# Routed layers of a transformer kernel: router products summed in one instruction, norm behind the gather, value blocks and head-wise exponentials on ScalarE, scores without key blocks

## The reference

```
weights = (x @ router_w)[..., 0] + router_b[0]            # (8, 512)
topv, topi = top_k(weights, 64); thr = topv[:, -1]
sel_mask = weights > thr
sel_idx = sort(topi[:, :63])                              # 63 tokens of each sequence
x_sel, pos_sel, w_sel, m_sel = the same tokens of x, position_ids, weights, attention_mask
hn = rmsnorm(x_sel, ln1)
q, kk, v = rope(heads(hn @ wq)), rope(heads(hn @ wk)), heads(hn @ wv)     # 16 heads of 16
a = softmax(q kk^T / 4 + m_sel)
x1 = x_sel + (a v) @ wo
x2 = x1 + gelu(rmsnorm(x1, ln2) @ w1) @ w2
out = x2 * w_sel at the selected places, 0 elsewhere, + x * (1 - sel_mask)
x = x_before + 0.5 * out
```

## Time and profile before

| | us |
|---|---|
| median of 3 runs | 2997.37 (2995.15 to 2999.2) |
| the profiled execution's own time | 3000.29 |
| its span in the profile | 2998.6 |
| first routed layer, from the first statistics to the last scatter addition | 1591.8 to 1814.4 |
| second routed layer, first block's places to the second norm | 2826.3 to 2944.3 |
| TensorE busy | 2496.2 |
| VectorE busy | 2165.9 |
| ScalarE busy | 1512.2 |
| GpSimd busy | 841.5 |

### The profile page before, as it was taken

One profiled execution on the slowest core, in us unless ns is written; L12 is line 12 of the kernel. 1 busy time (PEld: TensorE's weight loads), 2 busy tenths in 40 slices (PEclk: granted clock), 3 DMA queues, 4 the chain that ended last, 5 costly groups with the idle time before them and its releaser, 6 DMA issues. The chain is left out here.

```text
span 2998.6 us, 38823 instructions
## 1 busy us (share of the span) xinstructions
PE 2496.2 (83%) x13889; PEld 1335.8 (45%) x13889; DVE 2165.9 (72%) x3838; ACT 1512.2 (50%) x2213; POOL 841.5 (28%) x820
## 2 busy tenths in 40 slices
PE   6999999999899989899991576688888888885256
PEld 3444444444444444344440344355555555554134
DVE  3389688878889887979107564688878978873765
ACT  5655554546455545555551121377766766772111
POOL 3444343544444434444440000102211211221000
PEclk9999999999999999999995776799999999997678
DMA  5000000000000000000001001000000000001001
GB/s 162 24 1 1 1 1 1 1 1 1 1 1 1 1 1 1 1 1 1 1 1 48 15 1 36 1 2 2 2 3 2 2 3 2 1 2 49 14 1 57
DMA packets 29459, 33.07 MB, mean 11 GB/s; under 512 B 6568, under 2 KB 25704, under 8 KB 29272
## 3 DMA queue, kind: packets, MB, share of 16 engines
q1 hardware_dynamic: 28296, 28.02, 2.9%
q0 software_dynamic: 976, 2.56, 0.3%
HBM read 25.72 MB, written 4.19 MB: 10 GB/s over the span
## 5 line engine op out<-in xcount | busy, mean ns | idle before, releaser
L716 POOL TENSOR_TENSOR g_lo<-g_full,g_hi 128x512 f16<-128x512 f32 x512 | 658.4, 1289 | 912.0 <-ACT g_hi L788 910.4
L788 ACT ACTIVATE g_full<-hid,b_col 128x512 f32<-128x512 f32 x512 | 351.4, 686 | 562.1 <-PE hid L152 560.6
L150 PE MATMUL hid<-y_hi,w_hi 128*128 128x512 f16 x1024 | 396.3, 387 | 37.6 <-DVE y_lo L774 34.9
L151 PE MATMUL hid<-y_lo,w_hi 128*128 128x512 f16 x1024 | 395.7, 386 | 0.0
L152 PE MATMUL hid<-y_hi,w_lo 128*128 128x512 f16 x1024 | 395.2, 386 | 0.0
L150 PE MATMUL acc<-g_hi,w_hi 128*128 128x512 f16 x1024 | 389.2, 380 | 0.0
L151 PE MATMUL acc<-g_lo,w_hi 128*128 128x512 f16 x1024 | 389.1, 380 | 0.0
L152 PE MATMUL acc<-g_hi,w_lo 128*128 128x512 f16 x1024 | 388.9, 380 | 0.0
L788 ACT ACTIVATE g_hi<-hid,b_col 128x512 f16<-128x512 f32 x512 | 348.6, 681 | 0.0
L2027 DVE TENSOR_REDUCE mla_m_col<-mla_ps 128x1 f32<-128x512 f32 (+3 forms) x512 | 225.2, 484 | 66.1 <-PE mla_ps L1869 60.0
L2130 ACT ACTIVATE mla_p_full<-mla_ps 128x1280 f32<-128x1280 f32 x128 | 158.3, 1237 | 143.8 <-PE mla_ps L1899 143.5
(11 more groups left out here) (369 smaller groups left out, 4781.6 us busy)
## 6 DMA issues: line engine op xcount, KB each, us to landing
stage<-in_L_ffn_w_dram SPq DMA_DIRECT2D x16, 512.0 KB, 4.9
x<-in_L_attn_x_dram SPq DMA_DIRECT2D x8, 512.0 KB, 8.4
routed_w<-in_L_ffn_w_dram SPq DMA_DIRECT2D x4, 1024.0 KB, 8.5
out_dram<-x SPq DMA_DIRECT2D x8, 512.0 KB, 5.7
mla_sums<-mla_sum_row SPq DMA_DIRECT2D x128, 2.0 KB
mla_wq<-in_L_attn_Wq_dram SPq DMA_DIRECT2D x1, 1024.0 KB, 6.8
mla_wout<-in_L_attn_Wout_dram SPq DMA_DIRECT2D x1, 1024.0 KB, 9.1
routed_wqkv<-in_L_ffn_wq_dram SPq DMA_DIRECT2D x2, 256.0 KB, 3.7
```

The costliest lines, as they stand in the source:

```text
L150: pe.matmul(out, w_hi, v_hi, start=first, stop=False)
L151: pe.matmul(out, w_hi, v_lo, start=False, stop=False)
L716: pool.tensor_tensor(g_lo[:, g, :], g_full[:, g, :], g_hi[:, g, :], ALU.subtract).then_inc(tail_done, 1)
L788: act.activation(out[:, g, :], hid[:, ht % 4, :], ACT.Gelu, bias=b1_col[:, ht:ht + 1], scale=1.0 / WS).then_inc(gelu_done, 1)
```

## The change

In both routed layers:

- **Weighing.** VectorE multiplies the centred tile by the router column and sums it in one instruction (`accum_out`), 32 times, and multiplies the 32 sums by `rstd` afterwards. ScalarE normalizes all 32 tiles.
- **Blocks.** The first block ends with the copies of `slot_col` and `stay`. `one_hot`, the gather, the transposes of `one_hot` and the whole mask part move into the second block. GpSimd now zeroes `v_blk` and `qk` there and then issues the four mask gathers.
- **Norms.** Square and sum are taken pair by pair, right behind the copy of that pair's rows (first norm) or behind `add_selected` (second norm).
- **Order.** Values are projected before queries and keys, into shared banks. The mask pieces stand between the query and key projections on TensorE and between the rotations on VectorE.
- **Value blocks** are 16 ScalarE copies.
- **No key blocks.** `rotate` writes each head into a group of 32 rows with zeros in the other half; `turn_qk` makes eight transposes for a pair instead of four, both results are copied by ScalarE. `scores` makes 32 products for a pair, each of 16 rows by 64 columns.
- **Softmax.** The subtraction is gone: VectorE negates the maxima, ScalarE takes 16 exponentials of 64 elements for a pair with the maximum as bias and the sum as accumulated output. `softmax_shift` drains four banks of 256 elements; `scores` has one set of banks and waits for that drain.

Core of the diff:

```diff
-                    with dve.Fori(0, BATCH // 2) as two:
...
-                            dve.tensor_tensor(weighed[:, i, :, :], y[:, b, :, 0:D],
-                                              router[:, :].unsqueeze(1).to_broadcast([P, TILES, D]),
-                                              ALU.mult).then_inc(weigh_step, 1)
...
-                            dve.tensor_reduce(w_col[:, b, :], weighed[:, i, :, :], AX.X, ALU.add).then_inc(weigh_step, 1)
+                            if col >= 4:
+                                dve.wait_ge(weigh_step, col - 3)
+                            dve.scalar_tensor_tensor(weighed[:, t, :], x[:, b, t, :], ln_col[:, 3, col:col + 1], router[:, :],
+                                                     ALU.subtract, ALU.mult,
+                                                     accum_out=w_col[:, b, t:t + 1]).then_inc(weigh_step, 1)
+                    dve.tensor_tensor(flat_w, flat_w, rstd[:, :], ALU.mult).then_inc(weigh_step, 1)
...
+        def rms_square(dve, call, pr, src):
+            at = call * RMS_STEPS + 2 * pr
+            dve.tensor_tensor(sq[:, pr, :], src[:, pr, :], src[:, pr, :], ALU.mult).then_inc(rms_step, 1)
             dve.wait_ge(rms_step, at + 1)
+            dve.tensor_reduce(col[:, 0, pr:pr + 1], sq[:, pr, :], AX.X, ALU.add).then_inc(rms_step, 1)
...
         def scores(pe, pr):
+            if pr == 0:
+                pe.wait_ge(rot_step, 8 * PAIRS)
+            else:
+                pe.wait_ge(s_step, 6 * (pr - 1) + 4)
+            pe.wait_ge(qkt_out, 2 * (pr + 1))
+            for m in range(BLOCKS):
+                for i in range(2):
+                    toks = slice(i * ROWS, (i + 1) * ROWS)
+                    for c in range(4):
+                        rows = slice(32 * c, 32 * c + HEAD_DIM)
+                        last = pe.matmul(ps[toks, S_BANK + c, m * ROWS:(m + 1) * ROWS],
+                                         qk_t[rows, pr, m, toks], qk_t[rows, pr, BLOCKS + m, toks],
+                                         start=True, stop=True)
+            last.then_inc(s_done, 1)
...
-            dve.tensor_tensor(sv, sv, mx.unsqueeze(2).to_broadcast([P, HEADS, ROWS]), ALU.subtract).then_inc(s_step, 1)
+            dve.tensor_scalar(mx, mx, -1.0, None, ALU.mult).then_inc(s_step, 1)
...
             for m, (a, table) in enumerate(((0, cos), (1, sin), (0, sin), (1, cos))):
                 dve.tensor_tensor(r[m], src[:, :, a, :], table, ALU.mult).then_inc(rot_step, 1)
-            dve.tensor_tensor(out[:, :, 0, :], r[0], r[1], ALU.subtract).then_inc(rot_step, 1)
-            dve.tensor_tensor(out[:, :, 1, :], r[2], r[3], ALU.add).then_inc(rot_step, 1)
+            for a in range(2):
...
+                dve.tensor_tensor(out[:, :, :, 0:half], parts[0], parts[1], ALU.subtract).then_inc(rot_step, 1)
+                dve.tensor_tensor(out[:, :, :, half:2 * half], parts[2], parts[3], ALU.add).then_inc(rot_step, 1)
...
                 def exponential(pr):
-                    act.wait_ge(s_step, 4 * (pr + 1))
-                    act.activation(s[:, pr % 2, :, :], s[:, pr % 2, :, :], ACT.Exp).then_inc(s_exp, 1)
+                    act.wait_ge(s_step, 6 * (pr + 1))
+                    for hd in range(HEADS):
+                        last = act.activation(s[:, pr % 2, hd, :], s[:, pr % 2, hd, :], ACT.Exp,
+                                              bias=s_col[:, pr % 2, 0, hd:hd + 1],
+                                              accum_out=s_col[:, pr % 2, 1, hd:hd + 1])
+                    last.then_inc(s_exp, 1)
```

More of the change, by code:

```diff
@@ L1007, in _ @@
                     dve.wait_ge(small_in, 48)
-                    dve.tensor_copy(pos_rows_f[:, :], pos_rows[:, :]).then_inc(hot_step, 1)
-                    with dve.Fori(0, BATCH) as b:
+                    dve.tensor_copy(pos_rows_f[:, :], pos_rows[:, :]).then_inc(col_out, 1)
+                    for b in range(BATCH):
                         for t in range(TILES):
@@ L1193, in routed_layer @@
         proc_lo = sb("proc_lo", [P, PAIRS, D], F16)
+        hot_step = sem("hot_step")
+        gathered = sem("gathered")
+        sel_out = sem("sel_out")
+        hot_turned = sem("hot_turned")
+        hot_out = sem("hot_out")
+        mask_in = [keep.software(nc.semaphore(f"{tag}_mask_in{i}")) for i in range(PAIRS)]
+        mask_turned = sem("mask_turned")
+        mask_out = sem("mask_out")
+        mask_picked = sem("mask_picked")
+        mask_done = sem("mask_done")
         rms_step = sem("rms_step")
@@ L1273, in routed_layer, with select @@
         ANG_STEPS = 1 + 16
-        S_BANK, W_BANK = (6, 0, 6, 0), (2, 4, 2, 4)
+        QK_BANK = (3, 4, 5, 6)
+        V_BANK = (7, 7, 0, 0)
+        TURN_BANK = ((7, 0), (1, 2), (7, 0), (1, 2))
+        S_BANK = 3
         PUT_BANK = (2, 4, 6, 0)
-        def turn_qk(pe, pr):
-            pe.wait_ge(rot_step, 6 * (pr + 1))
-            for m in range(4):
-                last = pe.transpose(ps[:, 2 + pr, m * P:(m + 1) * P], qk[:, pr % 2, m * P:(m + 1) * P], ident[:, :])
+        def select(pe, pr):
+            for i in range(2):
+                for t in range(TILES):
+                    last = pe.matmul(ps[i * ROWS:(i + 1) * ROWS, 3 + pr, 0:ROUTED_EXT],
+                                     one_hot[:, pr, t, i, :], y[:, 2 * pr + i, t, :],
+                                     start=(t == 0), stop=(t == TILES - 1))
+            last.then_inc(gathered, 1)
@@ new lines, in turn_hot, with project_values @@
+        def turn_hot(pe, pr):
+            for t in range(TILES):
+                last = pe.transpose(ps[:, (7, 0)[pr % 2], t * P:(t + 1) * P],
+                                    one_hot[:, pr, t, :, :].rearrange("p i r -> p (i r)"), ident[:, :])
+            last.then_inc(hot_turned, 1)
+        def project_values(pe, pr):
+            for k in range(KD):
+                last = pe.matmul(ps[:, V_BANK[pr], (pr % 2) * D:(pr % 2 + 1) * D], h_t[:, k, pr * P:(pr + 1) * P],
+                                 wqkv[:, k, 2 * D:QKV], start=(k == 0), stop=(k == KD - 1))
+            last.then_inc(v_done, 1)
@@ new lines, in project_qk, with turn_mask @@
+        def project_qk(pe, pr):
+            for k in range(KD):
+                last = pe.matmul(ps[:, QK_BANK[pr], :], h_t[:, k, pr * P:(pr + 1) * P], wqkv[:, k, 0:2 * D],
+                                 start=(k == 0), stop=(k == KD - 1))
+            last.then_inc(qk_done, 1)
+        def turn_mask(pe, pr):
+            pe.wait_ge(mask_in[pr], 16)
+            if pr > 0:
+                pe.wait_ge(mask_out, pr)
+            for t in range(TILES):
+                last = pe.transpose(ps[:, 1, t * P:(t + 1) * P], mask_rows[:, pr, t * P:(t + 1) * P], ident[:, :])
+            last.then_inc(mask_turned, 1)
```

396 lines of the change are left out of this document (174 added, 222 removed).

## The result

The changed kernel takes **2929.52 us** (median of 4 runs, 2926.09 to 2929.82); the kernel before took 2997.09 beside it (4 runs, 2995.15 to 2999.2). The ratio is 0.977, with a 95% interval of 0.9758 to 0.9782. It is 67.6 us faster; 47 were forecast. The profiled execution took 2929.78, its span 2928.0.

A forecast was written before the change was run, and what follows sets the result against it. It took VectorE to bound the weighing and a chain of handovers between three queues, no engine full, the attention. Stage savings of 23.5 us a layer, 47 for two, took the median from 2997.4 to 2950 us, range 2922 to 2980.

The forecast's parts named there:

- A: Weighing in each routed layer, from the end of `shift` to the last sum: 26.0 us before, 10.4 us saved.
- 32 x 0.48: Weighing: 32 fused VectorE instructions at 0.40 us plus 0.08 for the summed output, 15.4 us.
- Rival 3: Weighing: the fused product runs at half rate, 0.27 us more 32 times, 8.6 us a layer; 2967 us, chance 0.09.
- B: Gather to first norm, from the places to `h` complete: 30.8 us before, 13.9 us a layer saved.
- C: First norm to the first scores: 25.1 us before, 28 after, 3 us a layer lost; mask work moves here.
- D: Attention, first scores to the last `add_selected`: 53.5 us before, 53 after, 0.5 us a layer saved.
- 16 exponentials in 6.4 us: Attention softmax: ScalarE's 16 exponentials for a pair at 0.40 us each, bounds 0.20 and 0.60.
- Scores in 3.7: Attention: a pair's 32 score products, 64 steps at 0.058 us, take 3.7 us; bounds 1.7 to 7.
- The walk: Attention stage stepped through instruction by instruction: 50 to 52 us; old lists gave 49.5 for 53.5, so 2 added: 53.
- E: Second norm: 6.6 us before; the last pair's square and sum cost 0.85 for 2.5, 1.7 us a layer saved.
- number 1: Attention: ScalarE's heads cost 0.25 us and scores may overlap, on average 10 us more a layer; 2930 us, chance 0.20.
- Rival 4: Attention: 16-row score products stall at 0.26 us a step, 16.6 us a pair; slower, 3040 us, chance 0.07.

## Why the prediction was right, and where it was not

The sign, the order of size and three of five stages were right. The forecast was 20.6 us short in the median. Between the profiled executions, whose spans differ by 70.6, 23.6 are missing: 15.0 in the stages of the sum, 8.6 outside them.

**A was mis-sized, by 2.4 us a layer.** The term was "32 x 0.48". I saw the accumulator read coming at its true duration and added it to the step; it runs beside the next product. The lower bound (12.8 us for the 32) was nearly the measured 13.0. The instruction's own duration is 0.48, and its kind in the earlier trace rows was read there as an average over 32, 0.40, which is the step. That row was the better price, whole. Rival 3 falls: the step of 0.407 us is that of the plain form, with both sources float32. The Trainium skill's sentence on half throughput (Vector Engine (DVE) Microarchitecture Reference, "Points that are easy to get wrong") is not borne out by this trace, for the summing form either.

**B was right in size**: saved 12.7 and 14.4 with the block's edge, for 13.9; the first layer is 1.2 off, just outside the bound of 1 us. `h` is complete 17.8 and 17.2 us after the places, for 16.5 in the sum; in the first layer the gather took 1.1 of that difference.

**C was right in its terms**: lost 2.6 and 4.2, for 3, and `rotate` 3 stood behind `turn_qk` 1, 1.35 us. That removing this wait brings nothing in the first layer, and 1.2 us in the second, was not foreseen; the transposes behind it wait for the last mask copy in any case.

**D failed, and two of its sizes were wrong.** "16 exponentials in 6.4 us" measured 5.3: 0.33 a head for my 0.40. At my own rate of 6 us per 0.1, that is 4 us. "Scores in 3.7" measured 0.91 at the high clock and 1.28 at the low: I took the value products as the nearest row, and these fill all 128 rows, where a score product fills 16. My lower bound of 1.7 ("row groups overlap") named the mechanism and was still too high. Put in by the experiment that undoes the overlap, the scores' term is 8 us a layer. Together that is 12 us in D, and only 5.5 to 6 came: TensorE stayed at the low clock for more of the stage than the 2 us that I had added for it, at 0.50 for 26 us on end. The experiment with the filled gaps gives that part as 5 to 7, so 3 to 5 more than I had; 1 to 4 us stay without a cause. The walk itself had warned: over the old lists it missed the trace by 4 us, and I added 2. So D was closer than its terms were because errors cancelled, which is luck. The Trainium skill (TensorE: Matmul & The Clock Gate, section "Why this matters for your kernels") has the rule that I should have weighed: products of few rows placed in different row groups run concurrently, 3.07 times as fast for four of them. The measured 3.2 and 3.5, between two orders of smaller products, lie near it.

**E was right**, 1.6 for 1.7.

**Outside the sum**: I took what lies around the routed layers as fixed. It gave another 8.6 us, 6.6 of them in the latent layer, whose cause the runs narrow down and do not find. The prediction has no term for it.

Of the rivals, number 1 (cheap heads with overlapping scores, 2930) named the measured time. Its mechanism was half right: the heads cost 0.33 and not 0.25, the scores did overlap, and A and the latent layer made up the rest. Rival 4 fell with the steps of 0.014 and 0.020 us; line 1706, on which it rested, keeps one shape of weights itself, and it is line 1709 behind it that brings the other.

## What to carry to other kernels

Price an instruction by its step in a run of its kind, start to start, not by its duration: a summed output was next to free on VectorE and cost 0.09 us on ScalarE. Splitting one ScalarE instruction over 1024 elements into 16 to save two VectorE passes of 1.2 us lost 11 us a layer, since it put ScalarE into the chain that TensorE waits for; look at who waits, and undo each part of a composite change once it is measured as a whole. Write products on few rows so that neighbours lie in different row groups (and banks), and where TensorE has to wait anyway in a short stage, useless transposes of 0.11 us in the gap can be worth more than they cost.

## What was not expected of the hardware

- 64 steps of 16-row products in 0.91 us, 14 ns each, and 46 ns each when the neighbours share a row group and a bank; 20 and 71 ns at the low clock.
- DVE_READ_ACCUMULATOR, 0.08 us, lies wholly beside the next instruction; ACTIVATION_READ_ACCUMULATOR, 0.19 us, adds 0.09 to each step.
- Granted clock 0.60 to 0.96 in one stage (0.84 in the second layer) by 106 transposes without use, 24 just ahead of it and 82 inside it; with those around the norms, 23.5 us of 2929.5 for the whole kernel.
- An untouched stretch of 5712 matmuls took from 939.2 to 950.7 us from kernel to kernel, not in the order of its starting time; in the long ones the granted clock was 0.87 to 0.89 for 0.93 or 0.94 at the same two places.
